# Cutting a weight transform's scratch traffic by hidden rows instead of by output columns

## The reference, cut to what matters

```python
x = layernorm(x + attention(x, Ws, Wa, Wo, bo))
hidden = silu(x @ W1.T) * (x @ W3.T)        # [.., 8192]
hidden = fwht(hidden) / sqrt(8192)
out = hidden @ W2.T                         # W2 is [2048, 8192]
x = layernorm(x + out)
```

## Time and profile before

| | us |
|---|---|
| median of 2 runs (5883.62 to 6010.39) | 5947.01 |
| the profiled execution | 5938.54 |
| its span, slowest core (core 7) | 5937.0 |
| the fastest core's span | 5838.6 |
| first DMA behind the transform's barrier | 1020.03 |

### The profile page before, as it was taken

How to read it: one execution, slowest core, us unless ns; L and a number is a source line. 1 busy time by engine, 2 the same in 40 slices (tenths; PEclk the granted TensorE clock), 3 DMA queues, 4 the chain that set the end, 5 groups by cost and what they waited for, 6 DMA issues and landing times.

```text
span 5937.0 us, 47049 instructions; the slowest of 8 cores (5838.6 to 5937.0 us)
## 1 busy us (share of the span) xinstructions
PE 3887.5 (65%) x17248; PEld 1740.7 (29%) x17248; DVE 898.6 (15%) x1961; ACT 494.3 (8%) x688; POOL 307.3 (5%) x480
## 2 busy tenths in 40 slices
PE   1111121546666656539999999999995938659594
PEld 0000000112333333214444444444442313223231
DVE  1211121023333121121101010101000010010102
ACT  1111111001110010000000000000000000010101
POOL 0000001110000000000000000000001111101010
PEclk7655565767778878759999999999987969878686
DMA  9888877672222333323232232222225455554443
GB/s 178 142 148 142 164 141 118 110 137 74 90 86 89 100 96 104 91 43 62 55 62 55 55 62 55 58 59 55 55 52 175 154 169 174 164 184 147 150 142 134
DMA packets 312895, 642.95 MB, mean 108 GB/s; under 512 B 19168, under 2 KB 187232, under 8 KB 299872
## 3 DMA queue, kind: packets, MB, share of 16 engines
q0 software_dynamic: 85328, 362.94, 28.1%
q1 hardware_dynamic: 227344, 277.00, 17.5%
HBM read 650.45 MB, written 167.77 MB: 138 GB/s over the span
## 4 chain that ended last, share of the span: by engine, by line
PE 57%; DMA 26%; DVE 5%; issue 5%; SPq 3%; another core or an unknown queue 2%; ACT 1%; POOL 1%; DVEq 0%; POOLq 0%; ACTq 0%
PE up L644 15%; PE up L655 15%; PE dps L753 14%; DMA vc<-vb 7%; DMA t2sb<-w2tmp 5%; PE sc L555 4%; PE av L487 4%; DMA w2tmp<-t1full 4%; DMA zz<-z2s 2%; SPq L253 2%; DMA w2p<-t2full 2%; DMA Hd<-hid 2%; DMA xsb<-xkT 2%; DMA zt<-zz 1%
## 5 line engine op out<-in xcount | busy, mean ns | idle before, releaser
L753 PE MATMUL dps<-w2h,Hd 128*128 128x512 bf16 x4096 | 969.0, 403 | 392.6 <-DMA w2h<-w2p 328.9
L644 PE MATMUL up<-y1t,w1b 128*128 128x512 bf16 x4096 | 942.8, 384 | 0.0
L655 PE MATMUL up<-y1t,w3b 128*128 128x512 bf16 x4096 | 940.3, 383 | 0.0
L753 PEld LDWEIGHTS dps<-w2h,Hd 128*128 128x128 bf16 x4096 | 417.1, 102 | 944.4 <-issue 606.3
L487 PE MATMUL av<-PT,vc 128*128 128x256 bf16 x2304 | 404.2, 336 | 268.4 <-DMA vc<-vb 236.6
L644 PEld LDWEIGHTS up<-y1t,w1b 128*128 128x128 bf16 x4096 | 404.6, 99 | 495.9 <-issue 50.1
L655 PEld LDWEIGHTS up<-y1t,w3b 128*128 128x128 bf16 x4096 | 404.2, 99 | 494.1 <-issue 46.8
L275 PE MATMUL pt<-t2sb,i2h_bf 128*128 128x512 bf16 x256 | 87.7, 462 | 685.1 <-DMA t2sb<-w2tmp 678.7
L670 DVE TENSOR_TENSOR hstg<-silu,up 128x512 bf16<-128x512 bf16 x256 | 176.1, 688 | 1623.6 <-PE up L644 962.0
L487 PEld LDWEIGHTS av<-PT,vc 128*128 128x128 bf16 x2304 | 248.8, 116 | 406.1 <-issue 343.2
L666 ACT ACTIVATE silu<-up 128x512 bf16<-128x512 f32 x256 | 152.8, 597 | 1636.0 <-PE up L644 1581.8
(11 more groups left out here) (91 smaller groups left out, 1397.1 us busy)
## 6 DMA issues: line engine op xcount, KB each, us to landing
w2h<-w2p POOLq DMA_DIRECT2D x128, 1024.0 KB, 6.6
vc<-vb SPq DMA_DIRECT2D x288, 256.0 KB, 2.7
rhs<-w2ch POOLq DMA_DIRECT2D x8, 4096.0 KB, 43.1
w2tmp<-t1full SPq DMA_DIRECT2D x8, 4096.0 KB, 45.3
t2sb<-w2tmp SPq DMA_DIRECT2D x16, 2048.0 KB, 14.4
w2p<-t2full SPq DMA_DIRECT2D x16, 2048.0 KB, 14.6
w1b<-w1tp POOLq DMA_DIRECT2D x64, 512.0 KB, 5.2
w3b<-w3tp POOLq DMA_DIRECT2D x64, 512.0 KB, 5.6
```

Of the source, the lines that this page charges most:

```text
L644: t.matmul(p1[:], bw1[:, k * 128:(k + 1) * 128], y1t[:, k * TQ + n * 512:k * TQ + n * 512 + 512], start=(k == 0), stop=(k == 15), skip_gro ...
L655: t.matmul(p3[:], bw3[:, k * 128:(k + 1) * 128], y1t[:, k * TQ + n * 512:k * TQ + n * 512 + 512], start=(k == 0), stop=(k == 15), skip_gro ...
L753: t.matmul(dps[dbase + m][:], Hd2[:, hh * FT2 + m * 128:hh * FT2 + (m + 1) * 128], buf[:, h2 * 512:(h2 + 1) * 512], start=(qb == 0 and h2 ...
```

## The change

The slices of the transform are cut along the hidden index instead of along D. T1 takes 8 of the 64 high indices at a time with all 2048 columns, and T2 takes 8 of the 64 low indices at a time with all 2048 columns. Sizes of loads, matmuls and evictions stay. What becomes different:

- `w2tmp` is [128, 64, 2048]. T1 still writes 32 KB in a row on each partition. T2 reads rows of 4096 bytes instead of 512.
- T2 of a slice needs all slices of T1, so all of T1 comes first, and then all of T2.
- T2's reads are issued by POOL instead of SP, into two buffers `t2sb` instead of one. The two halves still write one name.
- `t2full` is gone. Four evictions fill a staging buffer `stg` of [128, 2048] (two of them), which goes out in two writes of 256 KB (64 partitions, rows of 4096 bytes): 128 writes instead of 16, on the same semaphore `w2pw`. The two halves of a row again write one name, `w2p:{ll}`.
- The host lays W2 out in the new order.

```diff
-        d_tmp_s = d_tmp.rearrange("ch (s l) hi d -> ch s hi l d", s=2)
+        NHC = 8
+        d_tmp_s = d_tmp.rearrange("(s l) hi d -> s hi l d", s=2)
...
-            t2sb = [CT(nc.sbuf_tensor(f"t2sb_{i}", [128, 64, DC], BF16)) for i in range(1)]
-            t1full = [CT(nc.sbuf_tensor(f"t1full_{i}", [128, 64, DC], BF16)) for i in range(1)]
-            t2full = [CT(nc.sbuf_tensor(f"t2full_{i}", [128, 64, DC], BF16)) for i in range(1)]
+            t1full = CT(nc.sbuf_tensor("t1full", [128, 8, D], BF16))
+            t2sb = [CT(nc.sbuf_tensor(f"t2sb_{i}", [128, 8, D], BF16)) for i in range(2)]
+            stg = [CT(nc.sbuf_tensor(f"stg_{i}", [128, D], BF16)) for i in range(2)]
...
-            def emit_T2(ch):
+            def emit_T2(lc):
+                ti = lc % 2
...
                 for sh in range(2):
-                    E.op("sync",
-                         (lambda s, ch=ch, buf=buf, sh=sh: s.dma_start(
+                    E.op("gpsimd",
+                         (lambda g, lc=lc, buf=buf, sh=sh: g.dma_start(
                              out=buf[sh * 64:(sh + 1) * 64, :, :],
-                             in_=d_tmp_s[ch, sh])),
-                         reads=(f"tmpD:{ch}",),
-                         writes=("t2sb:0",), dma=f"tmpr{ch % 2}")
+                             in_=d_tmp_s[sh, :, lc * 8:(lc + 1) * 8, :])),
+                         reads=tuple(f"tmpD:{ch}" for ch in range(NHC)),
+                         writes=(f"t2sb:{ti}",), dma=f"tmpr{lc % 2}")
...
+                    lr, dq = c // 4, c % 4
+                    sg = stg[lr % 2]
                     if c % 2 == 0:
                         E.op("vector",
...
+                             (lambda h, dq=dq, ps=ps, sg=sg: h.tensor_copy(
+                                 sg[:, dq * 512:(dq + 1) * 512], ps[:])),
+                             reads=(f"pt2{c % 4}",), writes=(f"stg:{lr % 2}:{dq}",))
...
-                for sh in range(2):
-                    E.op("sync",
-                         (lambda s, ch=ch, d0=d0, sh=sh, t2b=t2b: s.dma_start(
-                             out=d_w2p_s[sh, :, :, d0:d0 + DC],
-                             in_=t2b[sh * 64:(sh + 1) * 64, :, :])),
-                         reads=tuple(f"t2f:0:{c}" for c in range(NSC)),
-                         writes=(f"w2p:{ch}",), dma="w2pw")
+                    if dq == 3:
+                        ll = lc * 8 + lr
+                        for sh in range(2):
+                            E.op("sync",
+                                 (lambda s, ll=ll, sh=sh, sg=sg: s.dma_start(
+                                     out=d_w2p_s[sh, :, ll, :],
+                                     in_=sg[sh * 64:(sh + 1) * 64, :])),
+                                 reads=tuple(f"stg:{lr % 2}:{q}" for q in range(4)),
+                                 writes=(f"w2p:{ll}",), dma="w2pw")
...
-                if ch >= 2:
-                    emit_T2(ch - 2)
-            emit_T2(NCH - 2)
-            emit_T2(NCH - 1)
+            for lc in range(NHC):
+                emit_T2(lc)
             E.barrier()
```

More of the change, by code:

```diff
@@ L166, in build_nc @@
     d_hid = nc.dram_tensor("hid", [64, 128, TQ], BF16, kind="Internal").ap()
-    d_tmp = nc.dram_tensor("w2tmp", [8, 128, 64, 256], BF16, kind="Internal").ap()
+    d_tmp = nc.dram_tensor("w2tmp", [128, 64, 2048], BF16, kind="Internal").ap()
     d_w2p = nc.dram_tensor("w2p", [64, 128, D], BF16, kind="Internal").ap()
@@ L215, in emit_load @@
                      writes=(f"rhs1:{ri}",), dma=f"w2in{ch % 2}")
[L217 to L222, removed]
-            def emit_T1(ch):
[L225 to L229, removed]
+            def emit_T1(ch):
+                ri = ch % 2
+                rflat = rhs1[ri].rearrange("p a b -> p (a b)")
+                t1flat = t1full.rearrange("p a b -> p (a b)")
                 for c in range(NSC):
@@ L244, in emit_T1 @@
                                  ps[:], FWSCALE, None, ALU.mult)),
-                             reads=(f"pt1{c % 4}",), writes=(f"t1f:0:{c}",))
+                             reads=(f"pt1{c % 4}",), writes=(f"t1f:{c}",))
                     else:
@@ L250, in emit_T1 @@
                                  ps[:], AF.Copy, scale=FWSCALE)),
-                             reads=(f"pt1{c % 4}",), writes=(f"t1f:0:{c}",))
+                             reads=(f"pt1{c % 4}",), writes=(f"t1f:{c}",))
                 E.op("sync",
-                     (lambda s, ch=ch, t1b=t1b: s.dma_start(
-                         out=d_tmp[ch], in_=t1b[:])),
-                     reads=tuple(f"t1f:0:{c}" for c in range(NSC)),
+                     (lambda s, ch=ch: s.dma_start(
+                         out=d_tmp[:, ch * 8:(ch + 1) * 8, :], in_=t1full[:])),
+                     reads=tuple(f"t1f:{c}" for c in range(NSC)),
                      writes=(f"tmpD:{ch}",), dma=f"tmpw{ch % 2}")
-            def emit_T2(ch):
-                d0 = ch * DC
-                buf = t2sb[0]
+            def emit_T2(lc):
+                ti = lc % 2
+                buf = t2sb[ti]
                 rflat = buf.rearrange("p a b -> p (a b)")
-                t2b = t2full[0]
-                t2flat = t2b.rearrange("p a b -> p (a b)")
                 for sh in range(2):
-                    E.op("sync",
-                         (lambda s, ch=ch, buf=buf, sh=sh: s.dma_start(
+                    E.op("gpsimd",
+                         (lambda g, lc=lc, buf=buf, sh=sh: g.dma_start(
                              out=buf[sh * 64:(sh + 1) * 64, :, :],
-                             in_=d_tmp_s[ch, sh])),
-                         reads=(f"tmpD:{ch}",),
-                         writes=("t2sb:0",), dma=f"tmpr{ch % 2}")
+                             in_=d_tmp_s[sh, :, lc * 8:(lc + 1) * 8, :])),
+                         reads=tuple(f"tmpD:{ch}" for ch in range(NHC)),
+                         writes=(f"t2sb:{ti}",), dma=f"tmpr{lc % 2}")
                 for c in range(NSC):
@@ L278, in emit_T2 @@
                                    skip_group_check=True)),
-                         reads=("t2sb:0", "i2h64_bf"),
+                         reads=(f"t2sb:{ti}", "i2h64_bf"),
                          writes=(f"pt2{c % 4}",))
+                    lr, dq = c // 4, c % 4
+                    sg = stg[lr % 2]
                     if c % 2 == 0:
                         E.op("vector",
-                             (lambda h, c=c, ps=ps, t2flat=t2flat: h.tensor_copy(
-                                 t2flat[:, c * 512:(c + 1) * 512], ps[:])),
-                             reads=(f"pt2{c % 4}",), writes=(f"t2f:0:{c}",))
+                             (lambda h, dq=dq, ps=ps, sg=sg: h.tensor_copy(
+                                 sg[:, dq * 512:(dq + 1) * 512], ps[:])),
+                             reads=(f"pt2{c % 4}",), writes=(f"stg:{lr % 2}:{dq}",))
@@ L286, in emit_T2 @@
                     else:
                         E.op("scalar",
-                             (lambda h, c=c, ps=ps, t2flat=t2flat: h.activation(
-                                 t2flat[:, c * 512:(c + 1) * 512], ps[:], AF.Copy)),
-                             reads=(f"pt2{c % 4}",), writes=(f"t2f:0:{c}",))
-                for sh in range(2):
-                    E.op("sync",
-                         (lambda s, ch=ch, d0=d0, sh=sh, t2b=t2b: s.dma_start(
-                             out=d_w2p_s[sh, :, :, d0:d0 + DC],
-                             in_=t2b[sh * 64:(sh + 1) * 64, :, :])),
-                         reads=tuple(f"t2f:0:{c}" for c in range(NSC)),
-                         writes=(f"w2p:{ch}",), dma="w2pw")
+                             (lambda h, dq=dq, ps=ps, sg=sg: h.activation(
+                                 sg[:, dq * 512:(dq + 1) * 512], ps[:], AF.Copy)),
@@ L299, in build_nc, with emit_vb @@
+            def emit_vb(ch):
+                E.op("gpsimd",
+                     (lambda g, ch=ch: g.dma_start(
+                         out=d_vb[ch * 128:(ch + 1) * 128, :],
+                         in_=d_xk[ch * 128:(ch + 1) * 128, :])),
+                     writes=(f"vb:{ch}",), dma=f"vbs{ch // 8}")
             emit_load(0)
             emit_load(1)
-            for ch in range(NCH):
+            for ch in range(NHC):
                 emit_T1(ch)
-                if ch + 2 < NCH:
+                if ch + 2 < NHC:
@@ L946 @@
     w2ch = np.ascontiguousarray(
[L947 removed]
+        W2.reshape(2048, 8, 8, 128).transpose(1, 3, 2, 0))
     H128 = _hadamard(128)
```

11 lines of the change are left out of this document (4 added, 7 removed).

## The result

The changed kernel is slower by 1.06%: the ratio to the kernel before is 1.0106, 95% interval 1.0084 to 1.0127. On the 5888.6 us that the kernel before took (median of 10 runs) that is 62 us. The others lie between 5936.8 and 5977.2 us.

A forecast was written before the change was run, and what follows sets the result against it. The prediction took the transform stage's transfers and the waits between them as the bound. T1 467 us, lead 22 and T2 515 summed to 1004 us against 1020, so 5922 us, predicted as 5920, range 5830 to 6030.

The forecast's parts named there:

- lead, two half reads in series: Wait before T2's first matmul: two half reads of 11 us each, 22 us, bounds 15 and 29.
- barrier: End of the transform stage, where the first load behind it starts: 1004 us against 1020 before.
- What bounds the kernel: Transform stage: its transfers and the waits between them bound it; nothing behind the barrier changes.
- Part 1: T1 first, without T2 beside it: 58 us a slice, last write landed at 467 us, up to 499.
- the ring of write and compute: T1's period counted as a 46 us write plus 12 us of matmuls and evictions: 58 us.
- Part 2: T2's reads, two halves in series: 11 us a half, between 7.5 and 14.4, lead 22 us.
- Part 3: T2's staged writes: 64 rows without overlap, 65.5 us a slice, 56 for the last, 515 us together.
- Its ring: A T2 row is evictions, first write, second write in series: 1.64 + 2L us, 7.05 in the quiet.
- The rival that two buffers would work: T2's staging rows overlap, leaving T2 bound by bytes: stage ends near 710 us, 5628 us in all; chance 0.03.
- L: Landing time of one 256 KB half-row write in T2: 2.7 us without other traffic, 4.7 beside a read.
- The range: Whole kernel: 5830 to 6030 us, taking in the sum's low end 5842 and high end 6021.
- The rival of slow writes throughout: T2's half-row writes take 4.7 us even without a read beside them: 6114 us in all; chance 0.15.

The follow-up runs named there:

- Experiment 6: Kernel before with all eight T1 first, then all T2, its own slices and rows kept; 5863 us, kernel before 5851 us beside it.
- experiment 7: Changed kernel with `w2tmp` padded to [128, 65, 2048], so a partition's writes lie 260 KB apart instead of 256; ratio 1.0070 to the kernel before.
- experiment 9: Changed kernel with full-height transfers, a semaphore per staging buffer, and vb DMAs moved behind T2's reads; 5682 and 5686 us, kernel before 5882.
- experiment 4: Changed kernel with one 4 MB read on 128 partitions a T2 slice instead of two halves, rows 4 KB; ratio 0.9998 to the kernel before.
- experiment 5: Kernel before with one full-height read and write a T2 slice instead of two halves each, rows 512 bytes; ratio 0.9759 to the kernel before.
- experiment 1: Changed kernel with different names for a staged row's two half writes, semaphore still shared; 5815 us, kernel before 5879 us beside it.
- experiment 2: Changed kernel with different names for the half writes and a semaphore for each of two staging buffers; ratio 0.9577 to the kernel before.
- experiment 10: Changed kernel with full-height reads issued by ACT instead of GpSimd, two slices ahead; ratio 1.0041 to the kernel before.

## Why the prediction was wrong

It forecast 16 us less and came to 62 us more. The 5951 us that this makes lie inside the stated range of 5830 to 6030 us, but the direction was wrong, and the range was wide enough to hold either. The place, the mechanism and the sign of each wait were right. The sum failed in its sizes, all in one direction:

| step | predicted | after (core 1) | off by |
|---|---|---|---|
| T1 until its last write has landed | 467 | 485.4 | +18 |
| lead, two half reads in series | 22 | 29.9 | +8 |
| T2's 64 rows | 515 | 571.8 | +57 |
| barrier | 1004 | 1087.1 | +83 |

*What bounds the kernel* was right: the transform's end moved by 63 us over the cores, and so did the time.

*Part 1* took 58 us a slice and said that both ways of counting, by bytes and by the ring of write and compute, gave it. The period was 60.4 us, and seven of them make 17 of the 18 us. Experiment 6 shows 58.1 with the old scratch layout and the same order. So the step missed what the new layout costs, 1 to 2 us a slice over the runs that have it: the 128 pieces of a write to `w2tmp` lie 256 KB apart now, and the load reads W2 in another order. Which of the two it is stays open, since experiment 7 didn't settle it. That bytes and ring agreed was in part chance: experiment 9 shows that the ring alone, without the vb, takes 56 us a slice.

*Part 2* put a half read in the middle of its two bounds, 11 us. It took 14.4 us, its upper bound. I had chosen the middle because the trace before couldn't tell short rows from half height. The rule of the Trainium skill that stood beside it ("SBUF — State Buffer", the DMA port swizzle: half the partitions reach half the ports) points the right way, and experiments 4 and 5 bear it out; its figure of about 218 GB/s is above the 161 and 168 GB/s that these reads moved (stretches 486 to 499 and 501 to 514 us of after), so even the 11.9 us estimated from it were too few.

*Part 3* is where most of the error lies. Its ring is exactly what the chain shows, and experiments 1 and 2 prove both of its waits: 137 us for the second half's and 159 to 168 us for the shared semaphore's. The rival that two buffers would work had 0.03, and it took a change of the code to bring it about. Three terms were mis-sized. L in the quiet was 2.87 us where I took 2.7, so a row was 7.27 instead of 7.05 us, 0.2 us in each of some 50 rows, 11 us in all. The reading time of a slice was 28.8 us instead of 26 (from 573.80 to the second half's issue at 588.70, and its median landing of 13.9). And beside a read I priced every write at 4.7 us. In truth the price is uneven: the write issued just behind a half read takes 10.5 to 10.9 us and the other 2.87, so two rows pass in these 29 us, not 2.4. This was the term that failed most: beside a read the four half writes of two rows take 27 us, where 4.7 us each would be 19. A slice is then 2 x 14.8 + 6 x 7.3 = 73.4 us, measured 73.7 on average, against 65.5. Seven times these 8 us are the 57 us by which the step was off.

*The range* took its upper end from the terms of T2 at their upper bounds, a barrier at 1103 us; T1 stayed at 467 us in it, though its own bound was 499. It came at 1087. The half reads were at their bound of 14.4 us; the two writes beside a read, (10.5 + 2.87) / 2 = 6.7 us on average, were beyond theirs of 6.0; T1, at 485, was over halfway to its own. That the barrier stayed below 1103 is mainly due to the writes in the quiet, a row of 7.27 us and not 7.84. The terms are not independent, since the reads' slowness is also the time for which a read stands in a write's way: if the rate stays low in one place, it does in the others.

*The rival of slow writes throughout* asked for L = 4.3 us on average. The average row was 571.8 / 64 = 8.9 us, so L was 3.7 on average, where the forecast's 515 us had 3.2. It went about halfway, by a few very late writes and not by slow ones throughout.

## What to carry to other kernels

Two buffers don't overlap while the wait for one counts all DMAs on a semaphore that both share, nor two transfers of different halves while they share one name: look in the chain for a write, an eviction and a write in turn, and count the waits, not the buffers. A transfer on 64 partitions took 14.4 us for 2 MB with rows of 512 bytes and of 4 KB alike, and one on 128 took 17 us for 4 MB; permuting the columns of a constant matrix was enough to get from one to the other. A difference of a few us is read on all cores before it is explained: the slowest one was the exception in experiment 7. When several terms of a sum hang on one unknown, move them together to their bounds before choosing a value in the middle.

## What the runs showed of the hardware

A transfer issued just behind a large one on another queue landed late in these runs. A write of 256 KB that takes 2.87 us alone took 10.5 us behind a half-height read that lasted 14.2, and with full-height reads of 17.3 us at the median two such writes in turn took some 7.3 us each (experiment 4). The engines were not idle meanwhile: their share was 0.85 from 575 to 585 us in the changed kernel. A write of 4 MB that takes 12.4 us alone took 42 to 47 us behind a load that took 30 us alone, with the engines at 0.94 (experiment 9). It was so behind GpSimd's queue and behind ACT's (experiment 10: up to 9.0 us). The Trainium skill ("DMA: Bandwidth & Descriptors", Queues, rings and completion order) says that each engine takes turns between its queues, but drains a whole packet before it switches, typically some 9 to 17 descriptors (the single pieces into which a transfer is cut). How many pieces of these reads and loads made up a packet no run here shows, so these landings neither confirm nor refute it, and why the writes are so late stays open.

The half reads of `w2tmp` took 13.7 to 14.3 us (medians of the cores) with 256 KB from partition to partition and 12.9 to 13.4 us with 260 KB (experiment 7).
